# Moving the QKV bias into TensorE and its evacuation to ScalarE, in a fused linear-attention and ternary-FFN layer

## The reference, cut to what matters

```python
# x: (8, 4096, 1024) f32
h   = layernorm(x)
qkv = h @ Wqkv + bqkv                      # 1024 -> 3072
q, k, v = split(qkv, 3)
q = q / norm(q);  k = k / norm(k)          # over the last axis
kv  = sum over tokens of k * v             # (1, 1024) per batch entry
x   = x + (q * kv) @ Wout + bout
# feed-forward, hidden 4096
h = layernorm(x) * ln1_g + ln1_b
h = gelu(h @ ternary(w1).T + b1)
h = layernorm(h) * ln2_g + ln2_b
x = x + h @ ternary(w2).T + b2
# ternary(w): scale = 1/mean(|w|); clip(round(w*scale), -1, 1) / scale
```

## Time and profile before

| | us |
|---|---|
| median of 2 runs | 2678.77 |
| the two runs | 2627.74 and 2729.8 |
| the profiled execution | 2635.73 |
| its slowest core, first to last instruction | 2634.2 |
| the other cores | 2603.3 to 2630.4 |

### The profile page before, as it was taken

One profiled execution on the slowest core, in us unless ns is written; L12 is line 12 of the kernel. 1 busy time (PEld: TensorE's weight loads), 2 busy tenths in 40 slices (PEclk: granted clock), 3 DMA queues, 4 the chain that ended last, 5 costly groups with the idle time before them and its releaser, 6 DMA issues.

```text
span 2634.2 us, 35308 instructions; the slowest of 8 cores (2603.3 to 2634.2 us)
## 1 busy us (share of the span) xinstructions
PE 1621.8 (62%) x10800; PEld 908.2 (34%) x10928; DVE 998.3 (38%) x2682; ACT 802.1 (30%) x1333; POOL 118.0 (4%) x217
## 2 busy tenths in 40 slices
PE   0254565453447235767767767767767767767767
PEld 0121222121123121434534534534534534534534
DVE  0456644443445213143243243243243243243243
ACT  0132256656664123312212212212212212212211
POOL 2111101111110000000000000000000000000000
PEclk9977777776778657888988988988988988988989
DMA  9875534555552670110010010010010010010000
GB/s 144 183 202 189 169 116 150 176 161 154 178 147 70 136 148 13 27 37 21 24 38 21 24 38 21 24 38 21 24 38 21 23 38 21 23 38 21 13 17 17
DMA packets 203594, 195.39 MB, mean 74 GB/s; under 512 B 160404, under 2 KB 160405, under 8 KB 203415
## 3 DMA queue, kind: packets, MB, share of 16 engines
q0 software_dynamic: 31200, 92.34, 12.7%
q1 hardware_dynamic: 157952, 67.18, 10.6%
q10 hardware_dynamic: 14264, 33.62, 3.5%
HBM read 117.55 MB, written 50.33 MB: 64 GB/s over the span
## 4 chain that ended last, share of the span: by engine, by line
PE 48%; DVE 13%; issue 9%; ACT 8%; DMA 7%; DVEq 7%; SPq 4%; ACTq 1%; POOL 1%; another core or an unknown queue 0%; POOLq 0%
PE py L690 18%; PE py L731 17%; PE pqkv L593 6%; DMA wstg<-w 6%; PE patt L672 3%; DVEq L963 2%; DVEq L806 2%; SPq L316 2%; DVE z1T L1063 2%; DVE outbuf L1047 2%; DVEq L1054 1%; DVE kvtmp L847 1%; SPq L310 1%; DVE xring L968 1%; ACT qhat L380 1%
## 5 line engine op out<-in xcount | busy, mean ns | idle before, releaser
L593 PE MATMUL pqkv<-wqkvp,h1T 128*128 128x512 bf16 x1505 | 401.4, 431 | 376.5 <-DVE qkvb L836 343.0
L690 PE MATMUL py<-w2p,h4buf 128*128 128x512 bf16 x1968 | 529.5, 398 | 134.5 <-DVE outbuf L1055 123.1
L731 PE MATMUL py<-z1T,w1p 128*128 128x256 bf16 x4096 | 482.3, 282 | 164.8 <-ACT h4buf L501 162.9
L731 PEld LDWEIGHTS py<-z1T,w1p 128*128 128x128 bf16 x4096 | 384.1, 101 | 263.6 <-issue 169.9
L593 PEld LDWEIGHTS pqkv<-wqkvp,h1T 128*128 128x128 bf16 x1536 | 163.4, 108 | 614.0 <-issue 480.0
L1005 DVE TENSOR_TENSOR h4sq<-h4buf 128x128 bf16<-128x128 bf16 x1024 | 222.5, 224 | 293.3 <-PE psumSQ L699 260.9
L501 ACT ACTIVATE h4buf<-py,beta1c 128x256 bf16<-128x256 f32 x512 | 240.5, 473 | 230.9 <-PE py L731 230.3
L1063 DVE CAST z1T<-pzT 128x128 bf16<-128x128 f32 x256 | 56.5, 282 | 581.6 <-PE pzT L711 581.6
L699 PE MATMUL psumSQ<-onesb,h4sq 128*128 128x1 bf16 x1024 | 167.5, 164 | 85.5 <-DVE h4sq L1005 85.5
L699 PEld LDWEIGHTS psumSQ<-onesb,h4sq 128*128 128x128 bf16 x1024 | 103.0, 101 | 227.3 <-issue 118.3
L696 PE MATMUL psumSQ<-onesb,h4buf 128*128 128x1 bf16 x1024 | 173.8, 170 | 0.0
(11 more groups left out here) (127 smaller groups left out, 1278.3 us busy)
## 6 DMA issues: line engine op xcount, KB each, us to landing
wstg<-w POOLq DMA_DIRECT2D x128, 512.0 KB, 6.0
xbufA<-x SPq DMA_DIRECT2D x32, 512.0 KB, 5.1
xbufB<-x SPq DMA_DIRECT2D x32, 512.0 KB, 3.4
out<-outbuf ACTq DMA_DIRECT2D x32, 512.0 KB, 2.6
h1scr<-h1buf ACTq DMA_DIRECT2D x32, 256.0 KB, 5.2
qhscr<-qhat ACTq DMA_DIRECT2D x32, 256.0 KB, 2.5
wqkvp<-wqkv POOLq DMA_DIRECT2D x8, 768.0 KB, 27.7
h1T<-h1scr SPq DMA_TRANSPOSE x256, 2.9
```

Of the source, the lines that this page charges most:

```text
L593: mm = te.matmul(out=pq[i % 4][:, :], lhsT=h1T[:, (g % 2) * 4096 + c * 512 + s * 128: (g % 2) * 4096 + c * 512 + (s + 1) * 128], rhs=wqkvp ...
L690: mm = te.matmul(out=py2[:, hh * 512:(hh + 1) * 512], lhsT=h4m, rhs=w2p[:, m * D + hh * 512:m * D + (hh + 1) * 512], start=(m == 0), stop= ...
L731: mm = te.matmul(out=py1[m % 2][:, :], lhsT=w1p[:, c * H + m * 128:c * H + (m + 1) * 128], rhs=z1T[:, c * 256:(c + 1) * 256], start=(c == ...
```

## The change

- The bias is no longer added at the evacuation. TensorE opens each of the 192 groups with an f32 one-row matmul, ones (1x128) by 512 values of `bqkv` (1x512), into the same bank; the eight bf16 matmuls add to it. `bqkvb`, its six broadcasts and VectorE's six copies of them are gone; `binit` and `abc` count 2 instead of 8.
- ScalarE evacuates, with six Copy activations at the head of `scA_back`. It waits first until `kv_acc` of the tile before is done (`akv`), then for each group; a drain follows, and both sums of squares come behind it, no longer between the evacuations.
- VectorE's `dvA_back` has only the reciprocals, kvtmp and `kv_acc`.
- Between the phases VectorE scales all eight blocks of `w1p` and all 32 of `w2p`; ScalarE scales none.

```diff
             def scA_back(u):
                 P = (u % 2) * 16
-                sc.wait_ge(aevac.h, 6 * u + 2)
+                if u >= 1:
+                    sc.wait_ge(akv.h, u)
+                for e in range(6):
+                    i = u * 6 + e
+                    sc.wait_ge(aqkv.h, i + 1)
+                    if e == 0 and u >= 1:
+                        sc.wait_ge(aqh.h, u)
+                    aevac.inc(sc.activation(out=qkvb[:, e * 512:(e + 1) * 512],
+                                            in_=pq[i % 4][:, :], func=AF.Copy))
+                sc.drain()
                 sc.activation(out=sqscrA[:, :], in_=qkvb[:, 0:D], func=AF.Square,
                               accum_out=stA[:, P + 8:P + 9])
                 sc.drain()
                 aqs.inc(sc.activation(out=stA[:, P + 9:P + 10],
                                       in_=stA[:, P + 8:P + 9], func=AF.Sqrt))
-                sc.wait_ge(aevac.h, 6 * u + 4)
                 sc.activation(out=sqscrA[:, :], in_=qkvb[:, D:2 * D],
                               func=AF.Square, accum_out=stA[:, P + 10:P + 11])
...
-            sc.wait_ge(bb1ev.h, 32)
-            sc.wait_ge(bg2.h, 1)
-            for c in range(4):
-                sc.activation(out=w1p[:, c * H:(c + 1) * H],
-                              in_=w1p[:, c * H:(c + 1) * H], func=AF.Identity,
-                              scale=g1m1c[:, c:c + 1])
-            w1s.inc(sc.drain())
-            sc.wait_ge(bb2.h, 1)
-            sc.wait_ge(w2t.h, 16 * 32)
-            for r in range(0, 32, 2):
-                sc.activation(out=w2p[:, r * D:(r + 1) * D],
-                              in_=w2p[:, r * D:(r + 1) * D], func=AF.Identity,
-                              scale=g2m2c[:, r:r + 1])
-            w2s.inc(sc.drain())
...
             te.wait_ge(smld.h, 16 * 6)
-            for e in range(6):
-                if e >= 2:
-                    te.wait_ge(binit.h, e - 1)
-                abc.inc(te.matmul(out=pq[e % 2][:, :], lhsT=onesrow[:, :],
-                                  rhs=rowsA[0:1, e * 512:(e + 1) * 512],
-                                  start=True, stop=True))
...
                         if i >= 4:
                             te.wait_ge(aevac.h, i - 3)
+                        te.matmul(out=pq[i % 4][:, :], lhsT=onesrow[:, :],
+                                  rhs=rowsA[0:1, e * 512:(e + 1) * 512],
+                                  start=True, stop=False)
                         for c in range(8):
                             mm = te.matmul(
                                 out=pq[i % 4][:, :],
                                 lhsT=h1T[:, (g % 2) * 4096 + c * 512 + s * 128:
                                          (g % 2) * 4096 + c * 512 + (s + 1) * 128],
                                 rhs=wqkvp[:, c * E3 + e * 512:c * E3 + (e + 1) * 512],
-                                start=(c == 0), stop=(c == 7))
+                                start=False, stop=(c == 7))
...
-            for e in range(6):
-                dv.wait_ge(abc.h, e + 1)
-                binit.inc(dv.tensor_copy(out=bqkvb[:, e * 512:(e + 1) * 512],
-                                         in_=pq[e % 2][:, :]))
...
             def dvA_back(u):
                 P = (u % 2) * 16
-                for e in range(6):
-                    i = u * 6 + e
-                    dv.wait_ge(aqkv.h, i + 1)
-                    if e == 0 and u >= 1:
-                        dv.wait_ge(aqh.h, u)
-                    if e == 2 and u >= 1:
-                        dv.wait_ge(akh.h, u)
-                    aevac.inc(dv.tensor_tensor(
-                        out=qkvb[:, e * 512:(e + 1) * 512],
-                        in0=pq[i % 4][:, :],
-                        in1=bqkvb[:, e * 512:(e + 1) * 512], op=ALU.add))
                 dv.wait_ge(aqs.h, u + 1)
...
-            bg2.inc(dv.drain())
-            for c in range(4, 8):
+            dv.drain()
+            for c in range(8):
                 dv.tensor_scalar(out=w1p[:, c * H:(c + 1) * H],
                                  in0=w1p[:, c * H:(c + 1) * H],
                                  scalar1=g1m1c[:, c:c + 1], scalar2=None,
...
             dv.drain()
-            for r in range(1, 32, 2):
+            for r in range(32):
                 dv.tensor_scalar(out=w2p[:, r * D:(r + 1) * D],
                                  in0=w2p[:, r * D:(r + 1) * D],
                                  scalar1=g2m2c[:, r:r + 1], scalar2=None,
```

More of the change, by code:

```diff
@@ L137, in build_program @@
     bcs = S("bcs"); bcsr = S("bcsr"); bpb = S("bpb"); bprep = S("bprep")
-    bg2 = S("bg2")
     bx = DSem(nc, es, "bx"); bqt = S("bqt")
@@ L153, in build_program @@
     wqkvp = sbA("wqkvp", [128, 8 * E3], BF16)
-    bqkvb = sbA("bqkvb", [128, E3], F32)
     xbufA = sbA("xbufA", [128, 2 * D], F32)
@@ L571, in _ @@
             te.wait_ge(smld.h, 16 * 6)
-            for e in range(6):
-                if e >= 2:
-                    te.wait_ge(binit.h, e - 1)
-                abc.inc(te.matmul(out=pq[e % 2][:, :], lhsT=onesrow[:, :],
-                                  rhs=rowsA[0:1, e * 512:(e + 1) * 512],
-                                  start=True, stop=True))
             for hh in range(2):
-                te.wait_ge(binit.h, 5 + hh)
                 abc.inc(te.matmul(out=pq[hh][:, :], lhsT=onesrow[:, :],
@@ L582, in _ @@
                                   start=True, stop=True))
-            te.wait_ge(binit.h, 8)
+            te.wait_ge(binit.h, 2)
             te.wait_ge(wqkvs.h, 128)
@@ L651, in _ @@
                                   start=True, stop=True))
-            te.wait_ge(w2s.h, 2)
+            te.wait_ge(w2s.h, 1)
             for r in range(32):
@@ L725, in _ @@
                 te.wait_ge(bze.h, 4 * p + 4)
-                te.wait_ge(w1s.h, 2)
+                te.wait_ge(w1s.h, 1)
                 for m in range(32):
@@ L757, in _ @@
                                       scalar1=0.5, scalar2=None, op0=ALU.mult))
-            for e in range(6):
-                dv.wait_ge(abc.h, e + 1)
-                binit.inc(dv.tensor_copy(out=bqkvb[:, e * 512:(e + 1) * 512],
-                                         in_=pq[e % 2][:, :]))
             for hh in range(2):
-                dv.wait_ge(abc.h, 7 + hh)
+                dv.wait_ge(abc.h, hh + 1)
                 binit.inc(dv.tensor_copy(out=boutb[:, hh * 512:(hh + 1) * 512],
@@ L1096, in build_program @@
         "mpre": 2, "mtot": 2, "mval": 2, "mbc": 2, "m1r": 1, "m2r": 1,
-        "abc": 8, "binit": 8, "kvc": 8, "kvw": 1, "bar": 5,
+        "abc": 2, "binit": 2, "kvc": 8, "kvw": 1, "bar": 5,
         "w1t": 128, "w2t": 512,
-        "bb1": 32, "bb1ev": 32, "w1s": 2, "bb2": 1, "bb2r": 1,
-        "bcs": 1, "bcsr": 1, "bpb": 4, "bprep": 1, "bg2": 1, "w2s": 2,
+        "bb1": 32, "bb1ev": 32, "w1s": 1, "bb2": 1, "bb2r": 1, "w2s": 1,
+        "bcs": 1, "bcsr": 1, "bpb": 4, "bprep": 1,
         "batt": 2 * NT, "bxp": NT,
```

## The result

The changed kernel takes 2860.4 us (median of 11 runs) against 2633.8 (10 runs of the kernel before): **1.088 times as long, 95% interval 1.084 to 1.091**. The prediction's 2835 stood 199 us above the profiled execution of the kernel before; the medians are 227 us apart, the two profiled executions (slowest core, 2634.2 and 2853.3) 219.

A forecast was written before the change was run, and what follows sets the result against it. Phase A was taken as bound by a chain of waits between engines; 186 (27 tiles) + 12 + 14.5 - 10.8 - 2.4 = +199 us gave 2835 us. Forecast's own range 2811 to 2878, 8-in-10 range 2795 to 2965.

The forecast's parts named there:

- The ring: Phase A: a chain of waits from engine to engine, one turn per tile, sets the time, not any engine's throughput.
- Start of the evacuation, +1.85: Per tile: ScalarE reaches the first bank only after h1buf, +1.92 us, less 0.07 for its faster copy.
- the fourth rival, the weight DMA: Phase A: ScalarE's 55.4 us wait for staged weights could shrink, at most -55 us, giving 2780; chance 6 in 100.
- Squares, +2.42: Per tile: sums of squares, now behind the sixth copy, make sixth evacuation to qhat 3.33 us instead of 0.91.
- Bias matmuls, +2.6: Per tile: two bias matmuls before e=4 and e=5 cost 1.7 and 0.9 us; bounds +1.7 to +4.2.
- Last five tiles, +26.5: End of phase A: two tiles +6.0 us each (+12), the last three, bound by TensorE, +4.8 each (+14.5).
- Set-up, -10.8: Program start: six copies of bqkvb gone, so VectorE's first statistics begin near 78.3 us instead of 89.08.
- Between the phases, -2.4: Scaling of W2's rows: VectorE alone needs 12.8 us, starting 1.4 later, against ScalarE's 16.73 for its half: -2.4.
- The low clock: Rival: TensorE stays at 1.2 GHz through phase A, a tile taking 30.8 us, total 2958; chance 14 in 100.
- The held clock: Rival: more work keeps TensorE at 2.4 GHz in phase A, a tile +3.4 us, total 2741; chance 6 in 100.
- table load: Rival: Copy needs another ScalarE table, two loads of 1.28 us per tile, +82 us, total 2917; chance 3 in 100.
- VectorE was not the bound: Rival judged: VectorE's throughput sets phase A's tile, so relief gains 125 and 13 us, total 2498; chance 3 in 100.

The follow-up runs named there:

- e1: The kernel before plus one-row f32 bias matmuls opening each group; VectorE still evacuates, by a copy without the add: 1.045 times the kernel before.
- e2: The changed kernel without its bias matmuls (bias of q, k and v left out), ScalarE still evacuating: 1.041 times the kernel before.
- e9: e6 with VectorE's and ScalarE's lists reordered and each tile's four weight chunks split into pairs before the squares and behind h1buf: 0.940 times the kernel before.
- e6: The kernel before with VectorE's eight broadcast copies moved behind its first statistics and all scaling between the phases on VectorE: 0.9971 times the kernel before.
- e5: The changed kernel with the f32 opening bias matmul over 128 rows instead of one: 1.063 times the kernel before.

## Why the prediction was right, and where its terms were off

*The ring bounds phase A.* Right. e1 and e2 each cost what they put on the ring, and e9, which beside e6's side parts only reorders, gains 6%.

*Start of the evacuation, +1.85.* Right: the first copy is 1.89 us after h1buf, the first add was 0.13 to 0.14 ahead: 2.0. The copy out of PSUM takes 0.60, as taken from the earlier trace rows. But the stretch from khat to the first evacuation grew only by 1.5 us in the first stage and 1.2 in the third: the fourth rival, the weight DMA, is real with some 16 us of its 55. ScalarE's wait for staged weights fell from 55.4 to 43.6 us, VectorE's in the tiles with sums from 24.7 to 15.5.

*Squares, +2.42.* Right: 3.36 against the 3.33 worked out.

*Bias matmuls, +2.6.* The mis-sized term: the pair grew by 3.6 us (10.59 against 6.96). The direction was right, the clock rises later with one-row matmuls at the head, but I took only the first of them at 1.2 GHz and a mean where there are two kinds of tile: 8.9 to 9.6 us, or 11.5 to 11.9 with TensorE at 1.2 GHz throughout, which is the upper bound (+4.2) and a little more. Nor was the form free of extra: 0.86 us taken from the earlier trace rows is 1.05 in front of full matmuls, and 1.71 is 1.97 (635.84 to 637.81). In 27 tiles this is 28 us too little; the weight waits above gave back some 16. So it is partly luck that the sum came as near as it did: two errors of opposite sign, the second one a rival that the sum had put at nothing.

*Last five tiles, +26.5.* Measured +35.6. In the last three it is the same extra: six groups of 2.88 us instead of 2.58 are 17.3 instead of 15.5. In the two before them TensorE was not at 2.4 GHz throughout, as I had supposed: the pair of tile 28 took 9.9 us, that of tile 27 6.6.

*Set-up, -10.8.* First statistics at 78.59 us, 10.5 earlier than the earlier trace rows:

```profile
78.59 1.21 DVE L788 TENSOR_REDUCE stA<-xbufA 128x1 f32<-128x1024 f32 x1
```

*Between the phases, -2.4.* From the start of w2's first column products to that of the second it is 29.9 us (1202.72 to 1232.64), where it was 32.8 (972.78 to 1005.57): -2.9. Timeline of the kernel before:

```profile
972.78 15.74 PE L642 MATMUL prow<-w2p,b2lc 128*1 128x512 bf16 x64 [37.92 <-DMA w2p<-wq2scr]
...
1005.57 16.41 PE L655 MATMUL prow<-w2p,onesb 128*1 128x512 bf16 x64 [13.51 <-ACTq L456]
```

and of the changed one:

```profile
1202.72 15.45 PE L630 MATMUL prow<-w2p,b2lc 128*1 128x512 bf16 x64 [38.99 <-DMA w2p<-wq2scr]
...
1219.72 12.76 DVE L917 TENSOR_SCALAR w2p<-w2p,g2m2c 128x1024 bf16<-128x1024 bf16 x32
1232.64 15.84 PE L643 MATMUL prow<-w2p,onesb 128*1 128x512 bf16 x64 [10.94 <-DVEq L921]
```

Together: the 199 of the prediction, plus 28 and 9 for the matmuls, plus 4 for the start, less 16: 224. The traces show 219.1: 226.2 in phase A, where these terms lie, and 7.1 less behind it, of which the prediction had 2.4.

*The rivals.* The low clock came true in part: in nearly half of the tiles (91 of 208) both groups on the ring are slow, and in 5 of this core's tiles the e=0 group behind them too, as above; from e=1 on TensorE is at 2.4 GHz in every tile, so TensorE, busy for 351.97 of the 558.38 us of the third stage, did not come to set the tile there. (The prediction's argument against this rival has a slip: at 1.2 GHz full-row matmuls would be two thirds of the 30.8 us, not three quarters.) The held clock did not: the granted clock of the third stage is 0.72 before and after. There is no table load with the copies: phase A of the changed kernel has one, at its first activation (L345, 5.6 us). VectorE was not the bound.

## What to carry to other kernels

Before work is moved off a busy engine, follow one turn of the chain and ask what the work covers and what it is covered by: here the engine that got relief (VectorE, 0.41 to 0.63 busy) bound nothing, and half of the loss was that the sums of squares stood behind the last copy rather than in the wait before it. On this ring the pieces added; where one engine was nearly full, mostly its own piece counted, so the same edit has another price after each other edit (8.8% on the ring, 3.6% in the reordered kernel). Where no engine is full (here none was over 0.63 in the tiles with sums and the quantizing ones), try the order of the lists first: it gave 6% with nearly the same instructions.

## What the runs showed of the hardware that was not expected

- An f32 matmul over one row at the head of a group of full matmuls costs 1.05 us of the stream at 2.4 GHz and 1.97 at 1.2 GHz for 512 columns; over 128 rows 0.86 (1004.42 to 1005.28 in e5) and 1.84 (605.67 to 607.51). The fuller matmul is the cheaper one.
- With one-row matmuls at the head of the groups TensorE stayed at 1.2 GHz through both groups before khat in 91 of 208 tiles, at the longest through 16 us of unbroken work; with 128 rows in none of 208, and in the tile shown it rose within 4.8 us.
- The granted clock shown for a stretch can mislead at the start of a program: it says 1.00 for 77 to 85 us, where a one-row f32 matmul takes 1.8 us, twice its later time.
